# First transfers reordered, experts' sums moved into the next attention block, the second unit's rows into the first unit, and the minima's transposes a half step later

## Time and profile before

| | us |
|---|---|
| median of 3 executions (2779.83 to 2784.29) | 2780.64 |
| the profiled execution | 2783.24 |
| its span | 2781.3 |

### The profile page before, as it was taken

One profiled execution on the slowest core, in us unless ns is written; L12 is line 12 of the kernel. 1 busy time (PEld: TensorE's weight loads), 2 busy tenths in 40 slices (PEclk: granted clock), 3 DMA queues, 4 the chain that ended last, 5 costly groups with the idle time before them and its releaser, 6 DMA issues. The chain is left out here.

```text
span 2781.3 us, 44323 instructions
## 1 busy us (share of the span) xinstructions
PE 2526.5 (91%) x16014; PEld 1387.9 (50%) x16014; DVE 1782.6 (64%) x4360; ACT 1398.0 (50%) x1921; POOL 748.4 (27%) x887
## 2 busy tenths in 40 slices
PE   5999988888999999997999997699999999887986
PEld 2444433333344444443889997334434434376553
DVE  2566676776777677774557775477777777455554
ACT  1444455445455555655348785155555555542332
POOL 3233333433311111100115664112221112124022
PEclk7999999999999999999899999699999999999999
DMA  5122222112132323220127776423222322001331
GB/s 168 45 49 70 56 54 69 36 44 52 52 94 67 101 72 90 76 63 12 50 69 212 222 218 152 86 59 84 80 84 71 89 78 62 3 8 24 93 88 40
DMA packets 102212, 218.54 MB, mean 79 GB/s; under 512 B 19116, under 2 KB 35372, under 8 KB 100716
## 3 DMA queue, kind: packets, MB, share of 16 engines
q1 hardware_dynamic: 93164, 203.66, 26.5%
q0 software_dynamic: 8832, 12.06, 2.4%
HBM read 100.34 MB, written 12.58 MB: 41 GB/s over the span
## 5 line engine op out<-in xcount | busy, mean ns | idle before, releaser
L1060 ACT ACTIVATE probT_a<-scores 128x1024 f32<-128x1024 f32 (+3 forms) x832 | 785.4, 949 | 722.9 <-PE scores L893 436.7
L1159 DVE CUSTOM_DVE_ANT_0 ring<-ring,maskb_a 128x512 f32<-128x512 f32 x1024 | 681.6, 719 | 182.4 <-PE ring L911 152.9
L911 PE MATMUL ring<-stacks_a 64*128 64x512 f32 (+7 forms) x1664 | 467.9, 414 | 72.7 <-DVE negm_a L1157 20.9
L932 PE MATMUL outputs<-probT_a,V_a 128*32 128x512 f32 (+6 forms) x3328 | 451.3, 587 | 18.7 <-ACT probT_a L1060 9.5
L1157 DVE TENSOR_REDUCE negm_a<-ring 128x1 f32<-128x512 f32 (+3 forms) x640 | 331.2, 563 | 170.7 <-PE ring L917 121.2
L872 PE MATMUL scores<-stacks_a 64*128 64x512 f32 (+7 forms) x1664 | 415.6, 479 | 0.0
L872 PEld LDWEIGHTS scores<-stacks_a 64*128 64x128 f32 (+1 forms) x1664 | 165.7, 187 | 439.2 <-issue 346.6
L911 PEld LDWEIGHTS ring<-stacks_a 64*128 64x128 f32 (+1 forms) x1664 | 237.4, 193 | 193.1 <-DVE negm_a L1159 77.2
L1203 DVE SCALAR_TENSOR_TENSOR parts_a<-ring,wcol,parts_a 128x512 fp32r<-128x512 f32 x112 | 84.1, 751 | 222.0 <-ACT parts_a L1107 222.0
L831 POOL TENSOR_SCALAR maskb_a<-ints_a 128x1024 bf16<-128x1024 int32 x32 | 116.4, 3639 | 393.1 <-DMA ints_a<-in_mask 362.0
L841 POOL TENSOR_TENSOR ve<-mv,epsilon 128x1 f32<-128x1 f32 x96 | 18.2, 189 | 740.5 <-DVE mv L1133 740.5
(11 more groups left out here) (237 smaller groups left out, 3763.8 us busy)
## 6 DMA issues: line engine op xcount, KB each, us to landing
stacks_a<-parts_a SPq DMA_DIRECT2D x672, 128.0 KB
raw<-in_moew SPq DMA_DIRECT2D x92, 512.0 KB, 4.0
ints_a<-in_mask SPq DMA_DIRECT2D x32, 512.0 KB, 3.4
swapped_a<-maskT_a SPq DMA_DIRECT2D x32, 256.0 KB, 3.5
wt<-in_w SPq DMA_DIRECT2D x7, 1024.0 KB, 4.9
kvT_a<-in_ctxT SPq DMA_DIRECT2D x12, 512.0 KB, 3.3
wrow<-in_row SPq DMA_DIRECT2D x7, 512.0 KB, 5.9
stacks_a<-narrow_a SPq DMA_DIRECT2D x224, 8.0 KB
```

The costliest lines, as they stand in the source:

```text
L911: last = pe.matmul(bank("S", j, n, e)[:, 0:w], Q[rows, g, qt * P:(qt + 1) * P], K[rows, g, 0:w], start=True, stop=not a.causal)
L932: last = pe.matmul(OB[x * slot:(x + 1) * slot, q0:S], V[:, m % 2, kb, c:c + slot], probT[:, kb % 2, x, q0:S], start=(kb == 0), stop=(kb == ...
L1060: act.activation(probT[:, kb % 2, 2 * p:2 * p + 2, q0:S], scores_bank(j, n)[:, :, q0:S], ACT.Exp, bias=0.0, scale=-1.0).then_inc(c_exp.sem, 1)
L1159: least = dve.tensor_tensor_reduce(sc, sc, maskb[:, m % 2, qt, :], 1.0, BIG * 2, ALU.add, ALU.min, out)
```

## The change

```diff
@@ timetable: m and mrows one step later (2 of 8 half steps; for heads of 32 the step is 1, as before)
-                (u * h, "split", 0, u + 1), (u * h + 1, "m", 0, u + 1), (u * h + 1, "mrows", 0, u + 1)]
+                (u * h, "split", 0, u + 1), (u * h + step, "m", 0, u + 1),
+                (u * h + step, "mrows", 0, u + 1)]
+FIRST = [(0, "x", 0), (0, "x", 1), (1, "c", 0), (1, "c", 1), (2, "q", 0), (3, "k", 0)]
@@ schedule: the second unit's first rows, out of the opening and into the first unit's first group
+                if k == base + 1 and (work, n) in [entry[1:] for entry in FIRST] and ahead == 2:
+                    continue
+            if m == base and len(units) > 1:
+                a = ATT[int(units[1][0][1:])]
+                for t, work, n in FIRST:
+                    if u * halves + h == t * halves // 8 and wanted(work, a, *units[1]):
+                        yield (work, base + 1, n)
@@ attention_block
+        routed = stages[0] == "a4"
+        def sums(b):        # 512 KB of probT, which is idle until the first exp
+            return probT[...][:, b * QT * D:(b + 1) * QT * D].rearrange("p (q d) -> p q d", q=QT)
+        early = oT[...][:, 0:2 * S].bitcast(I32).rearrange("p (q n) -> p q n", q=2)
+        def mask_half(j, n):
+            return early if routed and j == base and n == 1 else maski
@@ SyncE
-                sp.dma_start(X[:, QT:NT, :], tokens[:, QT:NT, :]).then_inc(c_x, 16)
-                weights(1)
-                sp.wait_ge(m_zero, 1)
-                sp.dma_start(total[0:NT * P, :]..., raw[:, :]).then_inc(m_cleared, 16)
-                sp.dma_start(total[NT * P:(NT + 2) * P, :]..., raw[:, 0:2 * D]).then_inc(m_cleared, 16)
             if not follows:
+                if routed:
+                    sum_load(0)
+                    for n in range(2):
+                        mask_load(base, n)
                 sp.wait_ge(c_fixed, number + 1)
                 sp.dma_start(stacks[ROW_HIGH:P:4, ...], same(fixed[0:32, 0, :], 2 * GS)).then_inc(c_static, 16)
+                if routed:
+                    for b in range(1, B):
+                        sum_load(b)
                 sp.wait_ge(c_static, 48 * number + 16)
                 ... (the two small transfers of constant rows, as before)
                 sp.wait_ge(c_static, 48 * (number + 1))
+            if first:
+                sp.dma_start(X[:, QT:NT, :], tokens[:, QT:NT, :]).then_inc(c_x, 16)
+                weights(1)
             for kind, j, n in work:
                 ...
+                if kind == "mrows" and j == 0:
+                    sp.wait_ge(m_zero, 1)
+                    (the two transfers of zeros to total)
                 if kind == "maskld":
+                    if routed and j == base:
+                        continue
@@ GpSimd: for the first unit (j == base) the count comes from VectorE
+                if j == base:
+                    pool.wait_ge(c_count, blk + 1)
+                    lengths_of(j, blk)          # lines 787 to 796, as before
+                    return
@@ ScalarE
+                    if routed and j == 4 * base and n == 0:      # before the first exp
+                        act.wait_ge(m_x, B)
+                    if routed and j == 4 * base:                 # before the first oT
+                        act.wait_ge(*c_maskb.at(base, 1))
@@ VectorE
+            if routed:
+                add_sums(0)                     # wait for the load, X += sums(0)
             dve.memset(mx[:, :, :, :].bitcast(F32), 0.0)
+                if kind == "len" and j == 0:
+                    dve.wait_ge(*c_rA.at("len", j, n))
+                    dve.tensor_scalar(energy[:, n, :], energy[:, n, :], 0.0, -1.0, ALU.is_equal, ALU.mult)
+                    dve.drain()
+                    dve.tensor_reduce(lens[:, n, 3:4], energy[:, n, :], AX.X, ALU.add).then_inc(c_count, 1)
+                    if routed and j == base:    # right after the copy of x(base, 1)
+                        for n in range(1, B):
+                            add_sums(n)
@@ routed block: the four loads (SyncE) and the four additions (VectorE) at its end are gone
-            for b in range(B):
-                sp.dma_start(xs(b), total[...]).then_inc(m_sum[b], 16)
-            for b in range(B):
-                dve.wait_ge(m_sum[b], 16)
-                dve.tensor_tensor(X[...], X[...], xs(b), ALU.add).then_inc(m_x, 1)
```

More of the change, by code:

```diff
@@ L575, in attention_block @@
                 c_kv.mark(j)
-            if kind == "maskld":
+            if kind == "maskld" and not (routed and j == base and n == 1):
                 c_mask.mark(j, n)
@@ L613, in stage_of, with mask_load, sum_load @@
             return st, b, att[st], int(st[1:]) % 2
+        def sums(b):
+            return probT[:, :, :, :].rearrange("p a g n -> p (a g n)")[:, b * QT * D:(b + 1) * QT * D]\
+                .rearrange("p (q d) -> p q d", q=QT)
+        early = oT[:, :, :].rearrange("p g n -> p (g n)")[:, 0:2 * S].bitcast(I32).rearrange("p (q n) -> p q n", q=2)
+        def mask_half(j, n):
+            return early if routed and j == base and n == 1 else maski
         @block.sync
         def _(sp):
+            def mask_load(j, n):
+                _, b, a, _ = stage_of(j)
+                sp.dma_start(mask_half(j, n)[:, :, :], io[f"mask{a.mask}"][b:b + 1, n * 2 * P:(n + 1) * 2 * P, :]
+                             .rearrange("o (q p) n -> p (o q) n", p=P))\
+                    .then_inc(c_early if routed and j == base and n == 1 else c_mask.sem, 16)
+            def sum_load(b):
+                sp.dma_start(sums(b), total[b * QT * P:(b + 1) * QT * P, :].rearrange("(q p) d -> p q d", p=P))\
+                    .then_inc(m_sum[b], 16)
             def weights(n):
@@ L705, in _ @@
                         sp.wait_ge(*c_ring.at("c", j - 1, 1))
-                    sp.dma_start(maski[:, :, :], io[f"mask{a.mask}"][b:b + 1, n * 2 * P:(n + 1) * 2 * P, :]
-                                 .rearrange("o (q p) n -> p (o q) n", p=P)).then_inc(c_mask.sem, 16)
+                    mask_load(j, n)
                 if kind == "mT" and n == QT - 1:
@@ L771, in first_query, with lengths_of @@
                                    selz[:, :].unsqueeze(1).to_broadcast([P, 2, 32]), ALU.mult).then_inc(c_qz.sem, 1)
[L773 to L786 removed]
+            def lengths_of(j, blk):
                 pool.tensor_scalar(lens[:, blk, 0:1], lens[:, blk, 3:4], float(S), None, ALU.add)
@@ L797, in lengths @@
                     .then_inc(c_pen.sem, 1)
+            def lengths(j, blk):
+                if j == 0 and blk == 0:
+                    pool.wait_ge(c_const, 96)
+                if j == base:
+                    pool.wait_ge(c_count, blk + 1)
+                    lengths_of(j, blk)
+                    return
+                pool.wait_ge(*c_rA.at("len", j, blk))
+                pool.tensor_scalar(energy[:, blk, :], energy[:, blk, :], 0.0, -1.0, ALU.is_equal, ALU.mult)
+                pool.drain()
+                n = S // 2
+                while n > 1:
+                    pool.tensor_tensor(energy[:, blk, 0:n], energy[:, blk, 0:n], energy[:, blk, n:2 * n], ALU.add)
+                    pool.drain()
+                    n //= 2
+                pool.tensor_tensor(lens[:, blk, 3:4], energy[:, blk, 0:1], energy[:, blk, 1:2], ALU.add)
+                pool.drain()
+                lengths_of(j, blk)
             for kind, j, n in work:
@@ L828, in _ @@
                 if kind == "maskcv":
-                    pool.wait_ge(*c_mask.at(j, n))
+                    if routed and j == base and n == 1:
+                        pool.wait_ge(c_early, 16)
+                    else:
+                        pool.wait_ge(*c_mask.at(j, n))
                     pool.wait_ge(*c_rD.at("S", 4 * (j - 2) + 3, halves - 1, 1))
-                    pool.tensor_scalar(maskb[:, j % 2, 2 * n:2 * n + 2, :], maski[:, :, :], 0.0, BIG, ALU.is_equal, ALU.mult)\
+                    pool.tensor_scalar(maskb[:, j % 2, 2 * n:2 * n + 2, :], mask_half(j, n)[:, :, :], 0.0, BIG, ALU.is_equal, ALU.mult)\
                         .then_inc(c_maskb.sem, 1)
@@ L1142, in _, with add_sums @@
                     .then_inc(c_selz, 1)
+            def add_sums(b):
+                dve.wait_ge(m_sum[b], 16)
+                dve.tensor_tensor(X[:, b * QT:(b + 1) * QT, :], X[:, b * QT:(b + 1) * QT, :], sums(b), ALU.add)\
+                    .then_inc(m_x, 1)
+            if routed:
+                add_sums(0)
             dve.memset(mx[:, :, :, :].bitcast(F32), 0.0)
```

26 lines of the change are left out of this document (6 added, 20 removed).

## The result

The changed kernel takes 2742.78 us (median of 4 runs, 2737.74 to 2747.51) against 2781.31 for the kernel before, measured beside it: ratio 0.9871, 95% interval 0.9851 to 0.9892, so 38.5 us less. Forecast were 22, and a range that ended at 2748: the sign was right, the size was not.

The account below looks back on a forecast made before the run. Chains of transfers and waits at attention block openings, with TensorE idle, were taken as the bound. Terms −4.3, 0, −4, −1, +2, +1.5, −12.2, −4 sum to −22.0 from 2783.24; less 2.6, 2759 us; range 2748 to 2772.

Parts of the forecast that it names:

- Start of a0: Opening of a0: constant rows issued earlier, ahead of the 3 MB, let S begin at about 39.6 us; −4.3 us.
- Key count: Opening of a0: the key count on VectorE is hidden behind transfers; 0, bounds +1 to −1 us.
- Sums and masks: Start of a4: experts' sums loaded behind the barrier and masks taken early bring the first minimum forward; −12.2 us.
- The second unit's rows: x, q and k leave the openings for a group of attention: −4 us in a0, −1 in a4, +2 in a6.
- m and mrows later: TensorE's 10.2 us of waits for the split go, partly replaced by waits for the ring's bank; −4 us.
- Clock: First two openings: without dense q and k first, attention half steps may run longer at the low clock; +1.5 us.
- Rival C: Minima's rows come late for ST in the 96 groups of the heads of 16: slower, 2801 us; chance 0.04.
- Rival A: Transfers only change places: S in a0 stays at 43.9, a4 gains only 8; sum −6.5, 2774 us; chance 0.13.
- Rival B: All covers hold and m frees TensorE, with m at −4: −35, 2746 us; chance 0.08.

Follow-up runs that it names:

- the slowed kernels: First of the two VectorE operations splitting the minima written twice: in the kernel before 2793.94 us, in that kernel with m and mrows a step later 2768.37 us.

## Why the prediction was wrong

By the medians of the parts run alone, and beside them what the steps said:

- Start of a0: −5.1; said −4.3. The landed times of the constant rows (said about 20, 19.18) and S (said 39 to 40, 38.56) were nearly right. The bytes ahead do delay the group's rows: S is at 34.9 without the second weights. The Trainium skill, "DMA: Bandwidth & Descriptors", section "Queues, rings and completion order", says that each DMA engine takes a queue's descriptors in ring order; S at 34.9 with 1.5 MB less ahead agrees with it. The first ST came at 63.38 and not at 67: with the transfers alone it is 10.5 us earlier where S is 5.6, and there the clock was at half for 27 us up to the first ST instead of 44.
- Key count: said 0; nothing at the start in the traces, open below 5 us.
- Sums and masks: −11.9 alone; said −12.2. The way there was partly wrong: the sums are loaded 7.8 us after the last scatter was issued and not some 4, right behind its landing, and TensorE's x, 13.0 us after it, gains only 0.6; said 4.3 (1740.5 to 1736.2). What the step rightly saw is the masks: the first minimum no longer waits for them, against 1742.24 above, and there the 9 us are, where the step had 12; that the −12.2 was met is partly luck.
- The second unit's rows: −2.0 alone and 0 inside the change; said −3. By the traces a6 was right (+2.3, said +2: its first ST 2 nearer and 4 back), the other two were not: a0 −1.2 (said −4), a4 −6.4 (said −1). In a4 I took the room that the 16 minima leave for the limit, and charged 5 us for coming back where 2.6 came.
- m and mrows later: −18.2 alone, +12.5 when taken back; said −4, bounds +2 to −10. **This is the step that failed:** it took the 10.2 us of waits for the split as all that hung on the old place. The runs showed a second wait there, 6.5 us at V's projection, and falls of the clock behind the longest waits.
- Clock: said +1.5, for the rows that leave the openings. It doesn't show: up to the start of a1 the changed kernel has 51.2 us at half rate with these rows moved and 51.2 without. As a whole the clock went the other way: in the first 79 us of before the granted mean was 0.72, in the first 63 of after 0.80, and over the span it rose from 0.947 to 0.956.

The parts alone add up to −37.2 against −38.5 measured. Of the 16.5 us missed, 14.2 are m's by this sum and 1.5 the clock's; by the run with m taken back m's are 8.5. The transfers and the sums were only put in alone and not taken out of the changed kernel, and each part has an interval of 6 to 11 us, so that the parts meet the whole so closely is partly luck.

The step failed in its reasoning as follows. I read 10.2 us in 17 places, took that as the most that could be won, and took 4 of it because a bank of the ring would be late next. The bank did become late, with 10.9 us in 19 places, and it cost little (0.2 us a unit in a2 and a3). The bound itself was wrong, twice. In the group above a wait of 1.26 us cost 2.34, since the clock fell behind it. And the minima's transposes at their old place made V's projection wait as well, 6.5 us in six places that stand in the list under another line. The total also hid where the waits are. In a4 and a5 seven waits stand in the second groups, 6.4 us, and these groups became 8.4 us shorter in the kernel with m later alone. In a0 and a1 there are nine, 3.7 us, and 12.0 were won by a2, of which 2.65 at the first ST. There V's projection had waited longer than the transposes (6.5 us against 3.7): without its wait the third groups of a0's first three units are 1.3 us shorter each, and they lengthen by as much when m is moved back. Part is clock (the records show 119 us at half rate up to a2 instead of 130), and how the rest divides into order and chance stays open. I had also not looked at what stood behind the waiting transposes in TensorE's queue: a projection, 2 us of ready work, which now runs in that gap.

Rival C (minima's rows late for ST) is refuted: by the trace of the changed kernel only one first ST of a group waits for its minima's rows, a6's first (2.32 us), and none in the middle of a block. The second groups of a2 and a3 are 0.6 us longer for another wait, as said above, and single groups of a1 that are longer by up to 1.7 us are not so with m later alone (a third group of 22.68, then 24.36, there 22.67). Rival A fell with S at 38.56 and with a4. Rival B had the right size nearly (2746), by luck: it took all bounds of the openings and left m at −4.

## What to carry to other kernels

Where TensorE is full, a wait of a microsecond in it can be worth more than its length, because the half clock can follow: read the group's length around the wait, not the total in a list of waits. Before pricing a wait, look at what stands ready behind it in the same queue, and which other waits of the list stand right behind the same instruction; a wait that can be moved behind ready work goes away even when another of the same total takes its place. A duration read in one row should be compared with its line's shortest and median: the split's 0.74 was the exception.

## What the runs showed of the hardware

**One VectorE operation, 0.18 or 0.74 us.** Line 1166 has a median of 176 ns and a longest of 740. In a4 and a5 it was 0.74 in four units in a row, each time beside GpSimd's 0.72 us product of line 846; in the whole span all 11 of the 112 that took over 0.3 us had a GpSimd instruction running beside them, and so had 16 of the 101 others. Here it starts 10 ns after GpSimd's and ends with it (VectorE's answer, then GpSimd's):

```profile
2069.23 0.74 DVE L1166 TENSOR_SCALAR mx_a<-negm_a 128x16 fp32r<-128x16 f32 x1
```

```profile
2069.22 0.72 POOL L846 TENSOR_TENSOR xh<-xh,wrow 128x256 f32<-128x256 f32 x1 [0.69 <-DVE xh L1264]
```

This is what made the split late in the longest waits. The Trainium skill, "SBUF — State Buffer", section "SBUF: two separate sides", says that a pair of ports is shared under an exclusive lock by GpSimd and by those VectorE instructions that run in a 2-port mode or have two inputs in SBUF (these only against a GpSimd instruction that reads SBUF); the one that starts first holds it for its whole instruction, and the other blocks. Line 1166 has one input, and no view shows its mode. The trace agrees with such a lock in these four places; the 16 short ones beside GpSimd show that running side by side is not enough. No kernel here moved line 846 away, so for line 1166 the cause is argued, not shown.

For the split's second operation, which has two inputs in SBUF, the slowed kernels show what the order does. In the kernel before it starts 0.03 us ahead of a GpSimd instruction of 0.73 us in the same four units, and takes 0.18 us. The doubled operation made it start 0.22 us behind that instruction, and in all four units, and in the same four with m later, it took 0.53 to 0.54 us and ended with it (slowed kernel, VectorE's answer, then GpSimd's):

```profile
1911.50 0.53 DVE L1170 SCALAR_TENSOR_TENSOR mx_a<-negm_a,mx_a 128x16 fp32r<-128x16 f32 x1
```

```profile
1911.28 0.72 POOL L848 TENSOR_TENSOR X<-xh,wrow 128x256 f32<-128x256 f32 x1
```

**A fall of the clock after a short wait.** From 1989.5 us, after 1.26 us of idleness, the granted clock was 0.52 over 3.5 us, which is the lower of its two levels (1.2 of 2.4 GHz), and it fell again behind the next unit's wait; these two groups took 20.95 and 20.98 us. Two others with the 0.74 us split took 19.42 and 19.37 without a fall. And in the unit after, one of 20.50 us had a fall behind a wait of only 0.44. So a fall does not follow each wait, nor only the long ones. Over the runs the longer wait had it more often: two of the four of 1.26 us here, three of four with m moved back, and all four of 1.87 us with the slower split.

**The start of a block takes its own time.** With the sums' loads moved behind the barrier, the first goes out 7.8 us after the last scatter was issued, where it had been 3.8. My step had put almost nothing there.
